# Third layer's edge stage: where VectorE reads an item's tile number, and which join releases the buffer of item records

## The chip, the cores and the metric

The kernel runs on one core of one Trainium2 chip. The metric is the device time of one execution in microseconds. A core has five engines that run side by side and synchronise by semaphores: TensorE (PE in the profile), VectorE (DVE), ScalarE (ACT), GpSimd (POOL) and SyncE (SP). In the stage of this case SP and POOL are used for starting transfers: SP starts plain ones, POOL the indirect ones (gathers), whose row addresses come from an index column in SBUF.

## The reference

The model is a graph network of four layers over 6250 nodes and 100000 edges, 128 features to a node. Each layer's output is added to its input and normalised. The case touches the third layer, of which only the edge part matters here:

```
row, col = edge_index
h = concatenate([x[row], edge_attr], axis=1)      # per edge: 128 + 128 features
h = relu(h @ w1a + b1a)                           # 256
h = relu(h @ w1b + b1b)                           # 256
h = h @ w1c + b1c
summed = segment_sum(h, col, num_segments=n)      # per node
```

The last product is linear, so the kernel sums the second hidden layer over the edges of a node first and multiplies by `w1c` in a later stage. The first product is split too: the part of `x` stands ready in one table (`table_layer2`, 256 values to a node), the part of `edge_attr` in another (`hidden_edge_parts`), and an edge only adds two rows.

## The kernel before

The edges are sorted by target node and laid out in *items*. An item holds up to four edges (S = 4) for each of 128 partitions, and a partition stands for one node of a tile of 128 nodes; all 128 nodes belong to tile number `j`, which the item's record carries in column `R_J`. The record (20 integers to a partition) also holds the indices of the item's gathers. The running sums of all 50 tiles lie in SBUF (`total`), and an item adds into the part of its tile. The stage goes through the items in a loop; a turn has U = 8 items, and the trip count is read at run time.

An item passes through five steps. In the text, "item g" counts from zero over all turns.

- **Fetch** (SP, L1992). The records of four items (called a *half-turn* below: a turn has two, `q` = 0 and 1) come in one transfer of 40 KB into `rec[q]`. There are two such buffers. The fetch for a buffer waits until the buffer is released.
- **Gather** (POOL, L2009 and L2014). One indirect DMA brings the edge parts of the item (`gh`, a ring of NH = 4 buffers), four more bring the node parts (`gx`, a ring of 8). Before the five, POOL waits for the record's fetch, for `turned` (the transposes of item g-8) and for `joined` (the join of item g-4).
- **Join** (DVE, L2081, helper `join`). Four additions of 128x256: `gx` += `gh`. It waits for the item's five gathers, and then increments `joined`.
- **Transposes, relu, layer 2** (PE L2035 in `turn_over`, ACT L2064 in `relu1`, PE L2045 in `layer2`). PE's order is the transposes of item g+1, then the four products of item g. PSUM has two buffers for each of the two steps, and so has `h1`.
- **Sum** (DVE, L2101). Eight `scalar_tensor_tensor` of 128x128 (max with minus the bias, then add to the running sum of tile `j`). DVE's order in the loop is: join of item g+2, read of item g's tile number into a register (`value_load`, L2096), wait for item g's products (`lin2`), sum of item g, and after the fourth item of a half-turn the release `rec_free[q]`.

The order on each queue is written out by hand; no planner is involved. The counters start above zero (`joined` by U, `turned` by U, `summed` and `act1` by 2) so that first uses of a ring pass.

Of the kernel before, what the change touches and what calls it, by code (L numbers as in the profile page):

```python
# [16 lines left out]
NT = -(-N // P)  # L17
# [7 lines left out]
U = 2 * B  # L25
# [28 lines left out]
R_POS, R_J, R_LIFT, R_SUM, FW = 0, 1, 2, 3, 4  # L54
# [12 lines left out]
def gnn(nc, xT, src, dst, windows, edges, W0, W0T, attI, attJ, probs, importance, bias0,  # L67
        Ws, WsT, Wd, WdT, attS, attD, bias1, bias1cols, w1a, b1a, w1b, b1b, w1cT, b1c, w2a, b2a, w2b, b2b,
        w3T, out):
    fp32, bf16, i32, u32, u16 = (mybir.dt.float32, mybir.dt.bfloat16, mybir.dt.int32, mybir.dt.uint32,  # L70
                                     mybir.dt.uint16)
    ALU, ACT, AX = mybir.AluOpType, mybir.ActivationFunctionType, mybir.AxisListType
    ds = bass.ds
    V, A, PE, G = nc.vector, nc.scalar, nc.tensor, nc.gpsimd
# [18 lines left out]
    with top:  # L93
        def sb(name, shape, dt=fp32, ctx=top):
            return ctx.enter_context(nc.sbuf_tensor(name, shape, dt))
# [6 lines left out]
        def sem(name):  # L102
            live.append(nc.alloc_semaphore(name=name))
            return live[-1]
# [18 lines left out]
        def flat(ap):  # L123
            return ap.rearrange("p a c -> p (a c)")
# [27 lines left out]
        with ExitStack() as ph:  # L152
            def carve(of, at, shape, dt=fp32):
                size = 1
                for k in shape:
                    size *= k
                words = size if dt in (fp32, i32, u32) else -(-size // 2)
                v = of[:, at:at + words]
                if dt is not fp32:
                    v = v.bitcast(dt)  # L160
                names = "abcd"[:len(shape)]
                v = v[:, 0:size].rearrange(f"p ({' '.join(names)}) -> p {' '.join(names)}", **dict(zip(names, shape)))
                return v, at + words
# [15 lines left out]
            for v in range(2):  # L179
                cbuf.append([])  # L180
                for half in range(2):
                    c, at = carve(pool1, at, [CB, REC], i32)
                    cbuf[v].append(c)
            fbuf = []
            for v in range(2):
                fbuf.append([])
                for half in range(2):
                    c, at = carve(pool1, at, [CB + IPC, REC], i32)
                    fbuf[v].append(c)
            we = []  # L190
            for v in range(2):
                c, at = carve(pool1, at, [QG, 2 * WIN], i32)
# [4 lines left out]
            for q in range(2):  # L197
                c, at = carve(pool2, at, [EC], i32)
# [65 lines left out]
            for v in range(STG):  # L264
                c, at = carve(flat(xr[:, :, :]), at, [T4, A0P])
                stage.append(c)
                c, at = carve(flat(xr[:, :, :]), at, [OWN])
# [576 lines left out]
        def turns(eng):  # L844

            return eng.value_load(trips[0:1, 0:1], min_val=1, max_val=GMAX // U - 7)
# [368 lines left out]
        with ExitStack() as att:  # L1215
# [10 lines left out]
            def room(at, *shape):  # L1226

                size = 1
                for k in shape:
                    size *= k  # L1230
                names = "abcd"[:len(shape)]
                v = big[:, at:at + size].rearrange(f"p ({' '.join(names)}) -> p {' '.join(names)}",
                                                   **dict(zip(names, shape)))
                return v, at + size
# [224 lines left out]
            for v in range(2):  # L1459
                c, at = room(at, H * (C + 1), SLOTS + 1)  # L1460
# [32 lines left out]
            for v in range(2):  # L1493
                c, at = room(at, CHUNKS[0], HID)
# [460 lines left out]
            with ExitStack() as ph:  # L1955
                NH, NQ = 4, 2
                Q = U // NQ
                rec = [sb(f"rec_m{q}", [P, Q, REC], i32, ph) for q in range(NQ)]
                gx, gh, h1, at = [], [], [], 0
                for u in range(U):  # L1960
                    v, at = room(at, S, HID)
# [4 lines left out]
                for v in range(2):  # L1966
                    c, at = room(at, 2 * S * P)
# [2 lines left out]
                psX = [pb(f"psX{v}", [P, 2 * 512], fp32, ph) for v in range(2)]  # L1970
                ps2 = [pb(f"ps2_{v}", [P, 2 * 512], fp32, ph) for v in range(2)]
                rec_in = [sem(f"rec_in_m{q}") for q in range(NQ)]
                rec_free = [sem(f"rec_free_m{q}") for q in range(NQ)]
                gathered = [sem(f"gathered_m{u}") for u in range(U)]
                gate, gate_v = sem("gate_m"), sem("gate_mv")
                joined = sem("edge_parts_added_m")
# [7 lines left out]
                def following(i, u):  # L1984

                    return (i, u + 1) if u < U - 1 else (i + 1, 0)

                @block.sync
                def _(sp):
                    def fetch(i, q):  # L1990
                        sp.wait_ge(rec_free[q], i + 1)
                        sp.dma_start(rec[q][:, :, :], rec_d[:, ds(i * U + q * Q, Q), :]).then_inc(rec_in[q], 16)  # L1992

                    n = turns(sp)
                    with sp.Fori(0, n) as i:
                        for q in range(NQ):
                            fetch(i, q)
                    fetch(n, 0)
# [74 lines left out]
                @block.vector  # L2073
                def _(dve):
                    def join(i, u):

                        dve.wait_ge(gathered[u], (i + 1) * 16 * (S + 1))
                        x_, e_ = flat(gx[u][:, :, :]), flat(gh[u % NH][:, :, :])
                        for s in range(S):
                            at = slice(s * HID, (s + 1) * HID)  # L2080
                            last = V.tensor_tensor(x_[:, at], x_[:, at], e_[:, at], ALU.add)  # L2081
                        last.then_inc(joined, 1)

                    for c in rec_free:
                        dve.sem_inc(c, 1)
                    dve.sem_inc(summed, 2)
                    dve.sem_inc(joined, U)
                    n = turns(dve)
                    join(0, 0)
                    join(0, 1)  # L2090
                    with dve.Fori(0, n) as i:
                        for u in range(U):
                            g, q = i * U + u, u // Q
                            join(*following(*following(i, u)))
                            dve.sem_inc(gate_v, 1)
                            j = dve.value_load(rec[q][0:1, u % Q, R_J:R_J + 1], min_val=0, max_val=NT)  # L2096
                            dve.wait_ge(lin2, g + 3)
                            for s in range(S):
                                for f in range(2):
                                    t = total[:, ds(j, 1), f, :].rearrange("p a n -> p (a n)")  # L2100
                                    V.scalar_tensor_tensor(t, ps2[u % 2][:, (f * S + s) * P:(f * S + s + 1) * P], nbb[:, f:f + 1], t,  # L2101
                                                           ALU.max, ALU.add)
                                last = V.drain()
                            last.then_inc(summed, 1)
                            if u % Q == Q - 1:
                                dve.sem_inc(rec_free[q], 1)

            fresh_semaphores()
            added = [sem(f"added_{s}") for s in range(S)]
# [1 line left out]
            with ExitStack() as ph:  # L2111
# [3 lines left out]
                for v in range(2):  # L2115
                    c, at = room(at, TB, P)
                    xd.append(c)
                    c, at = room(at, TB * P)
                    xdT.append(c)
                    c, at = room(at, 2, TB * P)  # L2120
# [174 lines left out]
        with ExitStack() as ph:  # L2295
            w3 = sb("w3T_", [P, D], fp32, ph)
            rec = [sb(f"rec_s{u}", [P, S, FW], i32, ph) for u in range(U)]
# [118 lines left out]
            with ExitStack() as fi:  # L2416
                FT = 7
                GF = groups(NT, FT)
                q = [[sb(f"q{v}{s}", [P, FT, D], fp32, fi) for s in range(S)] for v in range(2)]
# [226 lines left out]
```

## Time and profile before

| quantity | value |
|---|---|
| median of 3 runs | 8602.15 us (8601.02 to 8606.16) |
| span of the profiled execution | 9989.8 us |
| time of the profiled execution itself | not given beside the span |
| the stage of this case in the profile | 6224 to about 8160 us of the span |
| mean granted TensorE clock, whole span | 0.653 |
| busy in the span | PE 47%, DVE 51%, ACT 15%, POOL 58% |

The profiled execution is 1388 us longer than the median run, so a microsecond of the profile isn't a microsecond of the metric. The stage has 57 fetches, which makes 28 turns, 56 half-turns and 224 items. Slices 25 to 32 of the page's forty hold the stage. A granted clock of 1.0 is 2.4 GHz on TensorE, 0.5 is 1.2 GHz. "Idle before <-releaser" in a row is the time in which an engine did nothing before the instruction, and the program's name for what ended it; it is inferred from semaphore events, and "remote" or a transfer that ended long ago stands where no fitting event was found.

### The profile page before, as it was taken

The page shows a single profiled execution, that of the slowest core. Times are in us where ns is not written, and L with a number is a line of the kernel's source. Part 1 is how long each engine was busy: PE and PEld are TensorE (multiplying, and loading weights), DVE is VectorE, ACT ScalarE, POOL GpSimd, SP SyncE. Part 2 cuts the span into 40 slices and gives each one's busy share as a digit, 9 for nine tenths or more (in the row PEclk, how much of TensorE's full clock was granted, in tenths as well). Part 3 has the DMA queues.
Part 4 walks back from the last instruction along what each step waited for, and adds up shares of the span by engine and source line. Part 5 has one row for each costly group of instructions (what it writes and reads, how often), then busy time and mean ns, then how long its engine had stood idle before and what let it go on. Part 6 is the DMA issues. An engine that isn't in the chain of part 4 may idle for free. (4 is left out here: it accounts for less than half of the span.)

```text
span 9989.8 us, 82305 instructions
## 1 busy us (share of the span) xinstructions
PE 4658.3 (47%) x14536; PEld 2840.5 (28%) x14536; DVE 5136.0 (51%) x11795; ACT 1546.3 (15%) x3063; POOL 5819.3 (58%) x5427
## 2 busy tenths in 40 slices
PE   6287777733233322222322225566666566444443
PEld 5133333222222212221222122333333333333332
DVE  6387787755555444544454454444444433333333
ACT  1211111121111211111211112111111112000002
POOL 2466666536666466656466562555555534888885
PEclk8688888855555655555555555778778786555555
DMA  2432323443333233333333332444444441444445
GB/s 68 126 61 55 56 57 56 50 112 85 83 82 86 71 84 83 93 86 83 77 89 87 86 89 62 123 123 127 125 122 128 123 80 24 36 36 36 36 36 100
DMA packets 658400, 804.99 MB, mean 81 GB/s; under 512 B 289379, under 2 KB 496662, under 8 KB 657175
## 3 DMA queue, kind: packets, MB, share of 16 engines
q0 software_dynamic: 317424, 531.92, 26.9%
q1 hardware_dynamic: 340902, 272.29, 9.0%
q8 instruction: 22, 0.36, 0.0%
q14 instruction: 52, 0.42, 0.0%
HBM read 575.15 MB, written 228.61 MB: 80 GB/s over the span
## 5 line engine op out<-in xcount | busy, mean ns | idle before, releaser
L1767 POOL DMA_INDIRECT big<-table_layer,slot_records_L x2400 | 2325.7, 969 | 1615.9 <-DMA slot_records_L<-slot_records 861.3
L1786 PE MATMUL own_ps_L<-of_tile_L,big 50*128 50x16 f32 x1224 | 284.0, 370 | 2804.4 <-DVE fade_L L1871 2522.3
L2408 POOL DMA_INDIRECT sums_by_source<-msg,to x800 | 1252.4, 1565 | 260.7 <-issue 189.4
L981 POOL DMA_INDIRECT big<-table_layer,idx_L x912 | 951.1, 1043 | 619.5 <-issue 285.8
L2045 PE MATMUL ps<-big,w 128*128 128x512 f32 x1792 | 957.9, 685 | 341.6 <-ACT big L2064 208.4
L1786 PEld LDWEIGHTS own_ps_L<-of_tile_L,big 50*128 50x128 f32 x1224 | 272.0, 324 | 2879.5 <-issue 2865.1
L2014 POOL DMA_INDIRECT big<-table_layer,rec_m x904 | 877.5, 971 | 275.4 <-issue 272.0
L2101 DVE SCALAR_TENSOR_TENSOR big<-ps,nbb,big 128x128 f32 x1792 | 545.8, 346 | 914.0 <-remote 658.9
L1057 PE MATMUL sums_L<-h,ident 128*128 128x512 f32 x1344 | 716.4, 683 | 188.9 <-DVE h L1137 166.6
L1893 DVE TENSOR_TENSOR_SCAN big<-h,products_L 128x1122 f32<-128x1122 f32 x300 | 747.6, 2492 | 24.6
L2350 PE MATMUL psM<-h,same 128*128 x1600 | 413.8, 440 | 643.2 <-issue 640.1
L1778 PE MATMUL psH_L<-w,h 128*128 128x256 f32 x1584 | 671.8, 607 | 25.4 <-DMA h<-in_edges 25.4
L1844 DVE TENSOR_SCALAR of_tile_L<-slot_records_L,place 50x16 f32<-50x16 int32 x153 | 35.2, 230 | 1218.2 <-DMA slot_records_L<-slot_records 1128.6
L2009 POOL DMA_INDIRECT big<-hidden_edge_parts,rec_m x226 | 216.0, 956 | 688.0 <-DMA rec_m<-item_records 230.6
L1884 DVE TENSOR_TENSOR products_L<-products_L,big 128x512 f32<-128x512 f32 x600 | 613.5, 1067 | 0.0
L2045 PEld LDWEIGHTS ps<-big,w 128*128 128x128 f32 x1792 | 381.5, 225 | 766.9 <-issue 652.1
L2350 PEld LDWEIGHTS psM<-h,same 128*128 128x128 f32 x1600 | 355.9, 327 | 711.3 <-issue 711.3
L1778 PEld LDWEIGHTS psH_L<-w,h 128*128 128x128 f32 x1584 | 488.8, 319 | 138.0 <-issue 25.6
L2064 ACT ACTIVATE big<-psX 128x1024 f32<-128x1024 f32 x225 | 228.5, 1024 | 1704.5 <-DMA b<-in_b2b 1073.1
L1826 ACT ACTIVATE big<-psH_L 128x1536 f32<-128x1536 f32 (+1 forms) x144 | 193.7, 1345 | 1811.7 <-DMA h<-in_edges 860.0
L1057 PEld LDWEIGHTS sums_L<-h,ident 128*128 128x128 f32 x1344 | 289.5, 221 | 622.6 <-issue 606.3
L2035 PE MATMUL psX<-ident,big 128*128 128x128 f32 x1800 | 283.4, 308 | 391.9 <-DVE big L2081 303.4
(440 smaller groups left out, 7501.0 us busy)
## 6 DMA issues: line engine op xcount, KB each, us to landing
hidden_edge_parts<-big SPq DMA_DIRECT2D x72, 768.0 KB
hidden_edge_parts<-big SPq DMA_DIRECT2D x72, 640.0 KB
big<-table_layer,slot_records_L POOLq DMA_INDIRECT x2400
h<-in_edges SPq DMA_DIRECT2D x75, 384.0 KB
h<-in_edges SPq DMA_DIRECT2D x72, 320.0 KB
table_layer<-xr SPq DMA_DIRECT2D x49, 298.0 KB
big<-table_layer,idx_L POOLq DMA_INDIRECT x912
big<-table_layer,rec_m POOLq DMA_INDIRECT x904
```

The costliest lines, as they stand in the source:

```text
L981: G.indirect_dma_start(out=g[b][:, u, s, :], out_offset=None, in_=table, in_offset=bass.IndirectOffsetOnAxis(ap=at, axis=0)).then_inc(gath ...
L1057: PE.matmul(sums[b][u][:, 0:T * D], ident[:, :], prod[PROD[u]][:, s, :], start=(s == 0), stop=False, skip_group_check=True)
L1767: G.indirect_dma_start(out=ring[b][:, s, :], out_offset=None, in_=tab1_d[l], in_offset=bass.IndirectOffsetOnAxis(ap=fl[q][:, at + s, R_POS ...
L1778: last = PE.matmul(psH[:, c * HID:(c + 1) * HID], eT[b % 2][:, c * P:(c + 1) * P], w1[:, 1, :], start=True, stop=True)
L1786: last = PE.matmul(own_ps[:, c * SLOTS:(c + 1) * SLOTS], own1T[:, c * P:(c + 1) * P], of_tile[b % 2][:, :], start=True, stop=True)
L1884: last = V.tensor_tensor(p4[:, c, 0:C, 1:SLOTS + 1], bc(wt[:, hd, :], 1, C), ring[b][:, :, hd * C:(hd + 1) * C].rearrange("p s c -> p c s" ...
L1893: V.tensor_tensor_scan(flat(tot[b % 2][:, rows, :]), flat(shrink[:, rows, :]), flat(prod[:, :, :]), 0.0, ALU.mult, ALU.add)
L2014: G.indirect_dma_start(out=gx[u][:, s, :], out_offset=None, in_=tab2_d, in_offset=bass.IndirectOffsetOnAxis(ap=rec[q][:, a, s * FW + R_POS ...
L2045: last = PE.matmul(ps2[u % 2][:, f * S * P:(f + 1) * S * P], w2[:, k, f * P:(f + 1) * P], h1[u % 2][:, k * S * P:(k + 1) * S * P], start=( ...
L2101: V.scalar_tensor_tensor(t, ps2[u % 2][:, (f * S + s) * P:(f * S + s + 1) * P], nbb[:, f:f + 1], t, ALU.max, ALU.add)
L2350: last = PE.matmul(psM[v][:, s * P:(s + 1) * P], same[v][:, s, :], flat(h[:, ds(js[s], 1), :]), start=True, stop=True)
L2408: G.indirect_dma_start(out=sum_d[s], out_offset=bass.IndirectOffsetOnAxis(ap=to[u][:, s:s + 1], axis=0), in_=msg[u][:, s, :], in_offset=No ...
```

## The change

Each join copies the item's tile number out of the record into a small tile of its own (`tile`, one row of 8 integers), and the `value_load` before the sum reads that copy. The record is thereby no longer read after the join. The two `rec_free` semaphores go away. SP's fetch for buffer `q` of turn `i` now waits on `joined` for the fourth join of the items that used the buffer before. (`joined` starts at 8, so the count `i*U + q*Q + Q` is that of the join of item `(i-1)*8 + q*4 + 3`.) One drain of DVE stands between the first two joins and the loop.

```diff
                 rec = [sb(f"rec_m{q}", [P, Q, REC], i32, ph) for q in range(NQ)]
+                tile = sb("tile_m", [1, U], i32, ph)
...
-                rec_free = [sem(f"rec_free_m{q}") for q in range(NQ)]
...
                     def fetch(i, q):
-                        sp.wait_ge(rec_free[q], i + 1)
+                        sp.wait_ge(joined, i * U + q * Q + Q)
                         sp.dma_start(rec[q][:, :, :], rec_d[:, ds(i * U + q * Q, Q), :]).then_inc(rec_in[q], 16)
...
                         x_, e_ = flat(gx[u][:, :, :]), flat(gh[u % NH][:, :, :])
+                        V.tensor_copy(tile[:, u:u + 1], rec[u // Q][0:1, u % Q, R_J:R_J + 1])
                         for s in range(S):
...
-                    for c in rec_free:
-                        dve.sem_inc(c, 1)
                     dve.sem_inc(summed, 2)
                     dve.sem_inc(joined, U)
                     n = turns(dve)
                     join(0, 0)
                     join(0, 1)
+                    dve.drain()
                     with dve.Fori(0, n) as i:
                         for u in range(U):
-                            g, q = i * U + u, u // Q
+                            g = i * U + u
                             join(*following(*following(i, u)))
                             dve.sem_inc(gate_v, 1)
-                            j = dve.value_load(rec[q][0:1, u % Q, R_J:R_J + 1], min_val=0, max_val=NT)
+                            j = dve.value_load(tile[:, u:u + 1], min_val=0, max_val=NT)
...
                             last.then_inc(summed, 1)
-                            if u % Q == Q - 1:
-                                dve.sem_inc(rec_free[q], 1)
```

## Rows read from the trace of the kernel before

**Rows 1.** Windows view of the stage: its length, then busy time and count by engine.

```profile
core 0: us, PE busy (x) PEld busy (x) DVE busy (x) ACT busy (x) POOL busy (x), PEclk, DMA share, GB/s
6224.00:8170.00 1946.00, 1209.55 (x3614) 610.97 (x3614) 871.19 (x2704) 230.49 (x229) 1095.93 (x1135) 0.79 0.45 123
```

**Rows 2.** Waits of POOL in the stage: total us, times, longest us.

```profile
POOL big L2014 <- issue: 272.0, 893, 0.3
POOL big L2009 <- DMA rec_m<-item_records: 230.6, 25, 11.6
POOL big L2009 <- DVE big L2081: 211.0, 25, 9.1
POOL big L2009 <- PE psX L2035: 58.9, 5, 22.0
```

**Rows 3.** Groups of instructions by line in the stage (busy us, mean ns | idle before).

```profile
L2014 POOL DMA_INDIRECT big<-table_layer,rec_m x904 | 877.5, 971 | 275.4 <-issue 272.0 <-PE psX L2035 2.4 <-DVE big L2081 0.9
L2101 DVE SCALAR_TENSOR_TENSOR big<-ps,nbb,big 128x128 f32 x1792 | 545.8, 346 | 914.0 <-remote 658.9 <-PE ps L2045 166.2 <-issue 39.1
L2009 POOL DMA_INDIRECT big<-hidden_edge_parts,rec_m x226 | 216.0, 956 | 688.0 <-DMA rec_m<-item_records 230.6 <-DVE big L2081 211.0 <-issue 187.5
```

**Rows 4.** Timeline of one half-turn: start us, duration us, engine, line, operation [idle before].

```profile
6904.96 34.60 SPq L1992 DMA_DIRECT2D rec_m<-item_records  x2
6907.81 0.95 POOL L2009 DMA_INDIRECT big<-hidden_edge_parts,rec_m  x1 [9.06 <-DMA rec_m<-item_records]
6908.12 5.62 PE L2045 MATMUL ps<-big,w 128*128 128x512 f32 x8
6909.00 1.43 DVE L2081 TENSOR_TENSOR big<-big 128x256 f32<-128x256 f32 x4
6909.07 1.18 POOL L2014 DMA_INDIRECT big<-table_layer,rec_m  x1 [0.31 <-issue]
...
6913.91 2.66 DVE L2101 SCALAR_TENSOR_TENSOR big<-ps,nbb,big 128x128 f32 x8 [3.48 <-PE ps L2045]
...
6918.35 1.09 PE L2035 MATMUL psX<-ident,big 128*128 128x128 f32 x8 [0.29 <-DVE big L2081]
6919.27 3.60 PE L2045 MATMUL ps<-big,w 128*128 128x512 f32 x8
6919.30 2.66 DVE L2101 SCALAR_TENSOR_TENSOR big<-ps,nbb,big 128x128 f32 x8 [1.09 <-issue]
6919.60 0.95 POOL L2014 DMA_INDIRECT big<-table_layer,rec_m  x1 [0.30 <-issue]
...
6922.33 1.43 DVE L2081 TENSOR_TENSOR big<-big 128x256 f32<-128x256 f32 x4 [0.37 <-DMA big<-table_layer,rec_m]
...
6930.49 1.02 ACT L2064 ACTIVATE big<-psX 128x1024 f32<-128x1024 f32 x1 [14.81 <-DMA b<-in_b2b]
...
6932.46 0.96 POOL L2014 DMA_INDIRECT big<-table_layer,rec_m  x1 [0.31 <-issue]
6936.23 1.03 ACT L2064 ACTIVATE big<-psX 128x1024 f32<-128x1024 f32 x1 [4.72 <-DMA b<-in_b2b]
6936.27 2.66 DVE L2101 SCALAR_TENSOR_TENSOR big<-ps,nbb,big 128x128 f32 x8 [12.51 <-remote]
...
6941.78 0.95 POOL L2009 DMA_INDIRECT big<-hidden_edge_parts,rec_m  x1 [8.36 <-DVE big L2081]
```

**Rows 5.** Waits over the whole span, those on TensorE's results without a fitting releaser.

```profile
ACT big L2064 <- DMA b<-in_b2b: 1073.1, 87, 29.8
ACT big L1826 <- DMA h<-in_edges: 860.0, 48, 19.8
ACT big L1826 <- remote: 636.9, 39, 19.4
```

**Rows 6.** Instructions by line: the read of the tile number, and a DVE operation on one column.

```profile
L2096 DVEq TENSOR_LOAD <-rec_m x224: 298/302/318, 6247.7 to 8154.7; - x112
L2168 DVE TENSOR_SCALAR spare<-place x1: 140/140/140, 8160.4 to 8160.4; 128x1 f32<-128x1 f32 x1
```

## The prediction

> **What bounds the kernel now.** I looked at the windows first, to see the stage by itself: about 1940 us of the profiled span, with PE busy 1210, DVE 871 and POOL 1096 [rows 1]. No engine is full, so the next view is the waits of the engine that feeds the others. POOL starts 1130 gathers at 0.97 us each, with 0.305 us of issue between two (272.0 over 893) [rows 2, 3]. That is 1130 x 1.273 = 1438 us of work that can't be overlapped. The rest of the stage is POOL idle ahead of an item's first gather: 230.6 + 211.0 + 58.9 = 500 us [rows 2]; 1438 + 500 is the stage. There are 55 places between two half-turns, so some 9 us of pause stand in each.
>
> The timeline shows what a pause is [rows 4]. POOL starts the gathers of a half-turn at 6907.81 and ends the twentieth at 6933.42 (25.6 us). The next one starts at 6941.78, after 8.36 us. The two fetches in the view start 34.60 us apart, at 6904.96 and about 6939.2. Each is released by the sum of the fourth item of an earlier half-turn; here that sum starts at 6936.27, so it is the late part. It had waited 12.51 us. Its join was over at 6923.76, and the products that it needs (6919.27, 3.60 us) are drawn as ended at 6922.87. So the row says that DVE waited 12.5 us for something drawn as done. ACT does the same: transposes drawn as ended at 6919.44 release it at 6930.49. In total 658.9 us of DVE's waits at the sum are of this kind, 83 of them [rows 3].
>
> In the profile, then, the loop is: late products, fourth sum, fetch, pause of POOL. The question on which the prediction turns is whether the lateness exists in a plain run. The profiled span is 9989.8 us, and a plain run takes 8602.15: 1388 us are the profile's own, and they must lie somewhere. Late completions of TensorE are the best candidate, for two reasons. The same odd waits stand in another stage that has TensorE beside transfers (860.0 and 636.9 us at L1826) and in this one (1073.1 at L2064) [rows 5]. And TensorE has by far the most instructions here, 3614 loads and 3614 products beside 2704 on DVE and 1135 on POOL [rows 1], so whatever recording costs hits it first. The Trainium skill (Perfetto Trace Analysis, Per-instruction lifecycle) says that a TensorE row's end is estimated and not observed. By that the products may really have ended at 6936, which speaks for the second rival below; it doesn't tell whether a plain run has them so late.
>
> **The stage in a plain run, if the lateness is the profile's.** From the start of a half-turn's gathers (6907.81 = 0) by the rows [rows 4]: the join of its second item ends at 23.76 - 7.81 = 15.95. The fourth sum of the half-turn before may follow at once and takes 2.7: 18.7. The fetch that it releases brings POOL back to work after 6941.78 - (6936.27 + 2.66) = 2.85: 21.5. POOL itself is busy to 25.6 + 0.3 = 25.9. So the fetch is hidden with 4.4 us to spare, and the stage is POOL's 1438 us with or without the change. But TensorE counts: at the low clock transposes and products of an item take longer (5.62 beside 3.60 for the eight rows). Transposes at 10.5, then 2.0 and 6.8 (twice 1.09 and 3.60, less what overlaps), end the products at 19.3, the sum at 22.0 and the restart at 24.9: 1.0 us to spare, and none if TensorE comes into the half-turn with work left over. Also the fetch of the rows runs with no gather on the way, which wouldn't hold in a plain run.
>
> **The change part by part.**
> - *Release at the fourth join.* That join has ended at 6909.00 + 1.43 = 6910.43, 2.6 us after the start, where the fourth sum in the profile is done at 6938.9. With 2.85 us to the restart the record is there at 5.5, against 25.9 when POOL wants it: 20 us of cover, and no state of TensorE's clock can use it up. What is late next for POOL is the join of item g-4 (ended at 6918.21, so 10.4 against 25.9) and the transposes of item g-8. The join stands in DVE's queue behind the sum of item g-7, so TensorE's lateness still reaches POOL, though with three items of slack in place of one or two. Gain in a plain run: the low clock was granted in 2 x (1 - 0.79) = 0.42 of the stage [rows 1]; in these half-turns, 0.42 x 56 = 24, I take a remaining pause of 1 us, from 1.0 to spare less leftovers and the fetch's slower way: 24 us less 2 for what stays, 22. Bounds: 0 (always hidden), and the whole 500 less the first 22.0, about 480.
> - *The copy in the join.* 224 + 2 copies of one integer. The nearest row is 0.14 us [rows 6]: 32 us of DVE, which is idle for over 900 us of the stage [rows 3]. The copy comes before the additions, so it delays the join by up to 0.14, which eats into covers of 15 and 20 us. Nothing on POOL's path; if the cover is gone, 32 us. I take 0, since there is no gain to be had from it, and no wait is added.
> - *Reads from the copy.* The same load, 0.30 us in DVE's queue [rows 6], under the join's 1.43: 0.
> - *`rec_free` out, drain in.* Two increments a turn less (0.02 us class of instruction, not on a path), one drain in all: 0 within 1 us.
> - *SP.* The fetch's instruction moves forward and nothing is queued behind it but the next fetch. Its 40 KB come among gathers now, which take 0.45 of the transfer engines' time [rows 1]: a slower transfer, under 20 us of cover.
>
> There is one thing on the copy which a page has otherwise. In the rows a gather that meets a join takes 1.18 us rather than 0.95 [rows 4], so the two engines do get in each other's way. The Trainium skill (SBUF — State Buffer, SBUF: two separate sides) says that a DVE copy within SBUF can hold the ports that GpSimd needs to write descriptors, for its whole duration. As a mechanism here: each copy would hold POOL for its 0.14 us, 226 x 0.14 = 32 us, and POOL is the bound.
>
> Sum: 0.42 x 56 x 1 - 2 = 22 us less, all of it a plain run's time. 8602 - 22 = 8580.
>
> **The rivals.**
> 1. *All hidden already.* POOL never waits for a record in a plain run. For it: 4.4 us to spare at the high clock. Against: little to spare at the low one. Time 8602.
> 2. *TensorE is late in plain runs too, and by the transfers.* In the rows the last products are seen 3 us after POOL's last gather, so perhaps they come through only when the gathers have ended. Then unbroken gathers make TensorE the bound. From 6907.81 to 6936.27 three items got through, 9.5 us each, where the loop now needs 34.6 / 4 = 8.65. With no pause all 224 run at 9.5: 0.85 x 224 = 190 us slower, 8790. It decides if an item's products take over 8.65 us while gathers run. This is the slower side.
> 3. *The pauses are real, and lateness has nothing to do with the gathers.* Then the early fetch takes out a good part of 500 us. If everything, 8602 - 480 = 8122; if TensorE takes up most of it (busy 1210 plus a late 10 us each half-turn), some 2 to 4 us a pause go, 110 to 220 us: 8440.
> 4. *The copy is paid by POOL.* 32 us more on top of either of the first two: 8612 or 8634.
>
> **How the numbers follow.** Forecast (a remainder of pause goes, 8557 to 8592): 0.40. Rival 1: 0.32. Rival 3 in part: 0.10; whole: 0.06. Rival 4: 0.08. Rival 2: 0.04. A measurement of this kernel tells about 0.2%, 17 us, from no change. Faster: 0.32 of the forecast's 0.40 (a gain over 17), and rival 3: 0.48. Same: 0.08, rival 1, and half of rival 4: 0.44. Slower: the rest, 0.08. The range 8470 to 8625 holds the forecast, rival 1, most of rival 4 and the lower part of rival 3, some 0.8. The likeliest case's own range is 8557 to 8592.
>
> **What would show it.** In the profile after, SP's fetch follows the fourth join, some 28 us before POOL needs the record, and the wait `DMA rec_m` of 230.6 us is gone. If late completions are the profile's, the profiled stage needn't get shorter in proportion: POOL's idle time will be moved to waits for a join or for the transposes, and DVE's `remote` waits stay. A profiled stage near 1450 us with POOL gapless and a plain time near 8122 would show rival 3; gathers unbroken, POOL waiting on joins, and a plain time above 8625 rival 2. Gathers longer than 0.97 us in the mean by 0.03 or more would show rival 4. The forecast is wrong if the plain time moves by more than 45 us either way.

## The result, and the profile after

The kernel after takes 8671.6 us in the median (four runs, 8669.5 to 8675.1), the kernel before 8604.2 (8601.0 to 8616.3). The ratio is 1.0075 with a 95% interval of 1.0063 to 1.0086: slower by 0.75%, 67 us between the medians. The forecast was 8580, and the time lies outside the range of 8470 to 8625.

The profile of after has a span of 8673.4 us, which is its plain time. So a profile lengthens the run little or not at all (in the sets below the profiled run lies 0.2% from the median at most), and the profile of before with its 9989.8 us was no inflated picture of an 8602 us run; it was a picture of another one. The experiments showed what it most likely was: on one chip the kernel before takes 10106 us in the median of 17 runs, on two others 8598 to 8602. The times on record are of the second kind; the profile that the prediction read looks like the first, with the same waits. Its "late products" are real there and absent here. The rows of before that the rows of after should be held against are therefore those of a later profile of the unchanged kernel (e13), with a span of 8615.3 us.

First the windows view of the stage, kernel before and kernel after, on the kind of chip that counts. The columns are as in [rows 1].

```profile
5312.00:6800.00 1488.00, 1114.45 (x3632) 569.00 (x3632) 860.46 (x2704) 234.15 (x232) 1100.12 (x1135) 0.92 0.59 161
```

```profile
5309.00:6850.00 1541.00, 1125.16 (x3604) 571.07 (x3604) 866.69 (x2930) 231.87 (x228) 1172.05 (x1135) 0.91 0.57 156
```

Against [rows 1] the granted clock is 0.92 and not 0.79, and the stretch that holds the stage is 458 us shorter. Between the two fences one number moves with the time: POOL's busy time, 1100 to 1172 us for the same 1135 instructions. PE and DVE move by 11 and 6 us.

POOL's waits, before (first fence) and after (second), answer to [rows 2]:

```profile
POOL big L2014 <- issue: 269.3, 884, 0.3
POOL big L2009 <- issue: 204.8, 224, 136.7
POOL big L2009 <- DMA rec_m<-item_records: 14.3, 1, 14.3
```

```profile
POOL big L2014 <- issue: 273.3, 897, 0.3
POOL big L2009 <- issue: 204.3, 226, 135.8
```

Here the 500 us of [rows 2] have shrunk to one pause of 14.3 us (the 136 of L2009 is the wait ahead of the stage). That one is gone after: the early release does what it says. Now the groups by line, before and after, for [rows 3]:

```profile
L2014 POOL DMA_INDIRECT big<-table_layer,rec_m x904 | 882.1, 976 | 275.4 <-issue 269.3 <-DVE big L2081 2.7 <-PE psX L2035 2.1
L2101 DVE SCALAR_TENSOR_TENSOR big<-ps,nbb,big 128x128 f32 x1792 | 544.6, 345 | 123.2 <-PE ps L2045 68.7 <-issue 5.1
L2081 DVE TENSOR_TENSOR big<-big 128x256 f32<-128x256 f32 x904 | 326.0, 423 | 491.3 <-DMA big<-table_layer,rec_m 487.1 <-issue 2.2
```

```profile
L2014 POOL DMA_INDIRECT big<-table_layer,rec_m x904 | 954.1, 1055 | 275.5 <-issue 273.3 <-DVE big L2082 1.2 <-PE psX L2035 0.9
L2101 DVE SCALAR_TENSOR_TENSOR big<-ps,nbb,big 128x128 f32 x1792 | 542.4, 343 | 95.3 <-PE ps L2045 44.9
L2082 DVE TENSOR_TENSOR big<-big 128x256 f32<-128x256 f32 x904 | 318.3, 405 | 0.0
L2079 DVE COPY tile_m<-rec_m 1x1 int32<-1x1 int32 x226 | 32.0, 142 | 576.7 <-DMA big<-table_layer,rec_m 574.0 <-issue 0.8
```

The 904 gathers of node parts cost 72 us more: 976 to 1055 ns. The additions of the joins became *shorter*, 423 to 405 ns, though they still start 0.335 us apart. Something has changed in the join itself, and it was worth looking at single gathers. The account of the stage: from the first to the last of these gathers it takes 1453.6 us before (5317.3 to 6770.9) and 1511.4 after (5313.6 to 6825.0), 57.8 more, which is 72.0 of longer gathers less 14.3 of the pause. The two spans differ by 58.1 us, so the rest of the kernel plays no part.

The timeline shows how one gather gets long. In both kernels a join starts just ahead of a gather; before first, then after (columns as in [rows 4]).

```profile
5491.36 1.43 DVE L2081 TENSOR_TENSOR big<-big 128x256 f32<-128x256 f32 x4 [4.71 <-DMA big<-table_layer,rec_m]
5491.52 1.10 POOL L2014 DMA_INDIRECT big<-table_layer,rec_m  x1 [0.30 <-issue]
```

```profile
6017.67 0.14 DVE L2079 COPY tile_m<-rec_m 1x1 int32<-1x1 int32 x1 [4.72 <-DMA big<-table_layer,rec_m]
6017.74 1.41 DVE L2082 TENSOR_TENSOR big<-big 128x256 f32<-128x256 f32 x4
6017.82 2.17 POOL L2014 DMA_INDIRECT big<-table_layer,rec_m  x1 [0.30 <-issue]
```

Undisturbed, a gather takes 0.95 us. Before, this one loses 0.15 us. Its additions start at 0.00, 0.34, 0.68 and 1.01 of the join, the gather at 0.16; it gets on at the start of the second. After, it loses 1.22 us: from 6017.82 to about 6019.1, when the sum behind the fourth addition starts (6019.08). Both fit one picture: something early in a gather (an estimate from starts and losses: 0.04 us after its start) has to wait while DVE runs a join; with nothing ahead of the additions it gets in at the next start of one, 0 to 0.3 us later, and with the copy directly ahead it gets in only when all four are over.

That holds for most gathers and not for all. After, 198 of the 226 joins meet a gather that starts ahead of the fourth addition. In 175 of them the gather is held until all four are over, in 22 it gets in at an earlier start, and in one it loses nothing. One of the 22:

```profile
5426.75 0.14 DVE L2079 COPY tile_m<-rec_m 1x1 int32<-1x1 int32 x1 [0.21 <-DMA big<-table_layer,rec_m]
5426.82 1.41 DVE L2082 TENSOR_TENSOR big<-big 128x256 f32<-128x256 f32 x4
5427.66 1.06 POOL L2014 DMA_INDIRECT big<-table_layer,rec_m  x1 [0.30 <-issue]
```

This gather starts 0.84 us into the additions and loses 0.11 us, so it got in at the fourth. The difference seems to be VectorE's idle time ahead of the copy: 0.12 to 0.21 us in 21 of the 22, and 0.3 us or more in all 175. The traces of e5, e6 and e15 have the same split (after a short idle time 49 early and 5 held, after a longer one 1 early and 525 held). No run was made to test it, and it isn't a rule for every instruction: with the maximum of e8, 17 of 18 gathers were held after a short idle time too.

Gathers above 1.0 us number 101 of 1130 before and 221 after. In after, 156 of them lose 0.25 to 0.45 us, because 131 of the 226 joins start 0.2 to 0.3 us into a gather, so that the next one starts late in the join. A join is mostly woken by the landing of a gather (201 joins of before waited for one), which would explain why the phase repeats.

### The profile page after: what moved, and what is told of

It is laid out like the page before. It is cut to its first block and busy times, and to the rows that moved or that the text cites. A ratio compares the mean times of both kernels' runs of the same rounds, so it can differ in the third digit from the quotient of the medians.

```text
span 8673.4 us, 82502 instructions
## 1 busy us (share of the span) xinstructions
PE 4544.4 (52%) x14536; PEld 2796.5 (32%) x14536; DVE 5139.1 (59%) x12021; ACT 1537.5 (18%) x3063; POOL 5909.7 (68%) x5427
## 5 line engine op out<-in xcount | busy, mean ns | idle before, releaser
L981 POOL DMA_INDIRECT big<-table_layer,idx_L x912 | 975.4, 1070 | 405.3 <-issue 293.2
L2014 POOL DMA_INDIRECT big<-table_layer,rec_m x904 | 954.1, 1055 | 275.5 <-issue 273.3
L2045 PE MATMUL ps<-big,w 128*128 128x512 f32 x1792 | 890.9, 644 | 0.0
L2045 PEld LDWEIGHTS ps<-big,w 128*128 128x128 f32 x1792 | 359.0, 211 | 374.8 <-issue 374.8
L1856 DVE TENSOR_TENSOR z_L<-own_ps_L,big 128x64 f32<-128x64 f32 x150 | 39.2, 261 | 679.0 <-DMA big<-table_layer,slot_records_L 679.0
L2390 DVE TENSOR_TENSOR to<-away,rec_s 128x4 uint32<-128x4 f32 x200 | 33.1, 165 | 670.9 <-POOLq L2405 668.3
L1137 DVE TENSOR_TENSOR h<-sc_L,big 128x512 f32<-128x512 f32 x672 | 422.5, 689 | 0.0
```

Source lines behind the costliest of these rows:

```text
L981: G.indirect_dma_start(out=g[b][:, u, s, :], out_offset=None, in_=table, in_offset=bass.IndirectOffsetOnAxis(ap=at, axis=0)).then_inc(gath ...
L2014: G.indirect_dma_start(out=gx[u][:, s, :], out_offset=None, in_=tab2_d, in_offset=bass.IndirectOffsetOnAxis(ap=rec[q][:, a, s * FW + R_POS ...
L2045: last = PE.matmul(ps2[u % 2][:, f * S * P:(f + 1) * S * P], w2[:, k, f * P:(f + 1) * P], h1[u % 2][:, k * S * P:(k + 1) * S * P], start=( ...
```

## The experiments

| run | what it is | this, us | before beside it, us | ratio (95%) |
|---|---|---|---|---|
| e1 | before | 10110 (one) | 10106 | |
| e2 | copy, late release | 10112 | 10106 | 1.0005 (0.9987 to 1.0024) |
| e3 | early release, copy on ScalarE | 10030 | 10106 | 0.9907 (0.9882 to 0.9933) |
| e4 | after, second copy | 9950 | 10106 | 0.983 (0.980 to 0.986) |
| e5 | after | 8655.7 | 8601.8 | 1.0058 (1.0041 to 1.0074) |
| e6 | as e2 | 8663.7 | 8601.8 | 1.0067 (1.0050 to 1.0083) |
| e7 | as e3 | 8593.1 | 8601.8 | 0.9992 (0.9982 to 1.0001) |
| e8 | maximum in place of the copy | 8668.6 | 8601.8 | 1.0073 (1.0056 to 1.0090) |
| e9 | copy, drain, additions | 8606.2 | 8597.8 | 1.0012 (1.0003 to 1.0022) |
| e10 | additions, then copy | 8588.5 | 8597.8 | 0.9990 (0.9980 to 1.0000) |
| e11 | copy ahead of the wait | 8587.0 | 8597.8 | 0.9991 (0.9981 to 1.0000) |
| e12 | one copy per half-turn | 8609.0 | 8597.8 | 1.0014 (1.0005 to 1.0024) |
| e13 | before | 8617 (one) | 8599.1 | |
| e14 | before, memset written ahead of the additions | 8598.9 | 8599.1 | 1.000 (0.999 to 1.001) |
| e15 | after | 8660.9 | 8599.1 | 1.0072 (1.0055 to 1.0089) |
| e16 | as e11 | 8592.8 | 8599.1 | 0.9990 (0.9980 to 0.9999) |

Runs e1 to e4 were made on the chip where before takes 10106 us, the other twelve on two chips where it takes 8600 (e5 to e12 on one, e13 to e16 on the other).

**Taking the change apart.** Copy without release (e2, e6; the drain ahead of the loop is in them too, and left out in e3 and e7):

```diff
                         x_, e_ = flat(gx[u][:, :, :]), flat(gh[u % NH][:, :, :])
+                        V.tensor_copy(tile[:, u:u + 1], rec[u // Q][0:1, u % Q, R_J:R_J + 1])
...
-                            j = dve.value_load(rec[q][0:1, u % Q, R_J:R_J + 1], min_val=0, max_val=NT)
+                            j = dve.value_load(tile[:, u:u + 1], min_val=0, max_val=NT)
```

Release without a copy on VectorE (e3, e7), against the kernel after:

```diff
-                        V.tensor_copy(tile[:, u:u + 1], rec[u // Q][0:1, u % Q, R_J:R_J + 1])
...
+                        if u % Q == 0:                        # in relu1, ScalarE
+                            act.wait_ge(rec_in[q], (i + 1) * 16)
+                            A.activation(tile[:, q * Q:(q + 1) * Q], rec[q][0:1, :, R_J], ACT.Copy).then_inc(tiled, 1)
...
+                            if u % Q == 0:
+                                dve.wait_ge(tiled, i * NQ + u // Q + 1)
```

and a second copy into an unread tile (e4). On the first chip:

> The kernel before, unchanged, for a profile whose own time agrees with the plain time. Theory A (the copy keeps POOL from writing descriptors): the stage takes about 1470 us, POOL has no pause between half-turns, and its gathers take 0.96 to 0.97 us in the mean, so that all of them together are some 70 us shorter than in the kernel after (1.055 us for those of the node parts). Theory B (gathers are longer because nothing interrupts them, or because the fetch goes out among them; the copy is innocent): the gathers are short here only where POOL pauses, so pauses of one or more us stand between half-turns.

> The copy and the read from it as in the kernel after, but the buffer of records is released by the fourth sum, as before. Theory A: all of the loss is here, 8672 us (+0.8%), with gathers as long as after. Theory B: 8604 us, as before.

> The early release as in the kernel after, but the tile numbers are copied by ScalarE, one instruction of four numbers to a half-turn; VectorE does no copy. Theory A: the loss is gone, 8595 to 8606 us, gathers 0.97 us in the mean. Theory B: 8672 us as after, since the release is early here too.

> The kernel after with a second copy of the same number into a tile that nobody reads, behind the first. Theory A: POOL is held longer, by at least 0.14 us an item where a gather is under way: 8695 to 8740 us. Theory B: 8672 us, as after.

None of the times of theory A or B came out, since they were worked out for 8604 us and the kernel before takes 10106 here. But this chip is the one whose kind the first profile showed, so its rows can be held against [rows 2]. POOL's waits of the kernel before (e1), then of e3, then of e4:

```profile
POOL big L2009 <- DVE big L2081: 245.1, 27, 9.4
POOL big L2009 <- DMA rec_m<-item_records: 240.9, 26, 10.9
```

```profile
POOL big L2010 <- DVE big L2086: 400.4, 69, 10.6
```

```profile
POOL big L2010 <- DVE big L2084: 220.8, 30, 10.3
```

The pauses are there in e1, 486 us of these two waits. In e3 the wait for the record is gone, but the wait for a join has grown from 245 to 400 us, and the kernel is 76 us faster. The join stands behind a sum in VectorE's queue, and the sum waits for TensorE, so this is where the lateness would come back; it was argued from the code and not tested. With release and two copies (e4) the kernel is 156 us faster than before, although its gathers of node parts take 967.3 us against 881.6 in e1. The copy alone (e2) costs nothing that shows. POOL has slack here, and the copy also does less: the gathers are only 15 us longer than in e1 (896.5 us), as in 160 of e2's 226 joins the copy follows a sum within 0.25 us, the case in which few gathers are held. Why TensorE's results come late on this chip, and why e4 gains more than e3, I can't say; nothing was run for it, and the kernel after itself was not run on such a chip.

On the second chip:

> The kernel after, unchanged. The first four runs showed the kernel before at 10106 us on their chip, where the times on record are 8604 (before) and 8672 (after). Theory A with a second part (on a chip where TensorE's results come late, POOL pauses, and the early release helps; on one where they don't, POOL never pauses and only the copy's cost is left): where the kernel before takes 8604, this takes 8672; where it takes 10106, this takes 30 to 150 us less than before. Theory B: 0.8% slower on either.

> The copy and the read from it, with the release by the fourth sum as before. Theory A: where the kernel before takes 8604, this takes 8665 to 8680, with POOL's gathers 75 us longer in all; where before takes 10106, the same as before. Theory B: as before on either.

> The early release, with the tile numbers copied by ScalarE. Theory A: where the kernel before takes 8604, this takes 8590 to 8606 and its gathers 0.96 to 0.97 us in the mean; where before takes 10106, 10030 as it did. Theory B: 8672 on the first kind of chip.

On this chip the loss goes with the copy, as theory A has it, and B falls: the copy alone carries the whole loss (+62 us, e6, with 958.3 us for the 904 gathers), the early release alone gives 9 us (e7), with an interval that touches no change. In e7 nothing interrupts the gathers either, and the 904 take 883.4 us, so theory B's reason for longer ones is out. Of the times, e5 came out 16 us below what theory A gave and e6 1 us below its range. What A says of the kernel after on the slower chip stays untested.

**What kind of instruction.** e8 puts a maximum of the number with itself in the copy's place; e14 puts a memset there, in the kernel before.

```diff
-                        V.tensor_copy(tile[:, u:u + 1], rec[u // Q][0:1, u % Q, R_J:R_J + 1])
+                        r = rec[u // Q][0:1, u % Q, R_J:R_J + 1]
+                        V.tensor_tensor(tile[:, u:u + 1], r, r, ALU.max)
```

```diff
+                        V.memset(tile[:, u:u + 1], 0)
                         for s in range(S):
```

> The kernel after with a two-input maximum of the number with itself in place of the copy: same size, same place, another kind of instruction. Theory A in its narrow form (only a copy takes the second pair of ports that GpSimd writes its descriptors through): where before takes 8604, this takes 8600 to 8615. Theory A in its wide form (any instruction ahead of the additions lengthens what VectorE runs without a break, and gathers wait for its end): 8660 to 8680.

> The kernel before with one thing more: a memset of one integer of a tile that nobody reads, directly ahead of the four additions; release and read of the tile number are untouched. Theory C: it is enough that a short instruction runs straight into the additions, whatever it reads: 8655 to 8680 us where before takes 8600. Rival E: the instruction has to read SBUF (the copy and the maximum do): 8600 to 8612. Where before takes 10100, no difference that the intervals can tell.

The maximum costs what the copy costs (+67 us, gathers 961.2 us in all), so it isn't a matter of copies. The memset costs nothing, and the additions and the gathers keep their old length:

```profile
L2015 POOL DMA_INDIRECT big<-table_layer,rec_m x904 | 879.6, 973 | 275.5 <-issue 267.9 <-DMA rec_m<-item_records 3.7 <-DVE big L2083 3.0
L2083 DVE TENSOR_TENSOR big<-big 128x256 f32<-128x256 f32 x904 | 324.4, 421 | 482.2 <-issue 482.2
```

So theory C, by which any short instruction there is enough, was too wide. But e14 isn't as clean a test of rival E as it was meant to be. The profile doesn't draw the memset ahead of the additions:

```profile
5475.48 0.42 DVE L2083 TENSOR_TENSOR big<-big 128x256 f32<-128x256 f32 x1 [4.45 <-issue]
5475.49 0.06 DVE L2080 MEMSET tile_m<- 1x1 int32 x1
5475.53 1.19 POOL L2015 DMA_INDIRECT big<-table_layer,rec_m  x1 [0.30 <-issue]
```

In 189 of the 226 joins the memset starts 0.01 us behind the first addition, in the other 37 0.01 us ahead of it. The copy and the maximum start 0.07 us or more ahead of it in every join. So either the instruction has to read SBUF (rival E), or it only has to hold the additions back by its 0.07 us; these runs don't tell the two apart.

**Where it stands.** e9 puts `dve.drain()` between copy and additions, e10 moves the copy behind the additions (it then increments `joined`), e11 and e16 move it ahead of the wait for the gathers, e12 copies four numbers at once in the first join of a half-turn.

```diff
+                        dve.wait_ge(rec_in[u // Q], (i + 1) * 16)
+                        V.tensor_copy(tile[:, u:u + 1], rec[u // Q][0:1, u % Q, R_J:R_J + 1])
                         dve.wait_ge(gathered[u], (i + 1) * 16 * (S + 1))
                         x_, e_ = flat(gx[u][:, :, :]), flat(gh[u % NH][:, :, :])
-                        V.tensor_copy(tile[:, u:u + 1], rec[u // Q][0:1, u % Q, R_J:R_J + 1])
```

> The kernel after with a drain between the copy and the four additions. The traces so far (before at 8602 on that chip) show a gather that starts during a join waiting for the next start of an addition where nothing stands ahead of them, and for the end of all four where a copy or a maximum stands directly ahead. Theory C (what counts is that the small instruction runs straight into the additions, which then give no opening to POOL): with the drain between them the gathers go back to 0.97 us in the mean; 8590 to 8615 us where before takes 8602. Theory D (the small instruction costs POOL by itself, or its presence in the join does): 8655 to 8680, as after.

> The kernel after with the copy behind the four additions instead of ahead of them (it carries the increment of joined). Theory C: nothing stands ahead of the additions, so 8590 to 8620 us where before takes 8602, unless the sum that may follow straight after the copy takes its place. Theory D: 8655 to 8680.

> The kernel after with the copy ahead of the wait for the gathers, so that VectorE's idle time (208 of 226 joins in the kernel after have one, 2.8 us in the mean) lies between copy and additions. Theory C: 8590 to 8612 us where before takes 8602. Theory D: 8655 to 8680.

> The kernel after with one copy of four numbers in a half-turn's first join, none in the other three. Both theories: a quarter of the loss, on top of what the early release gives (8593 with the copy on ScalarE): 8593 + 65 / 4 = 8609, 8603 to 8620 us where before takes 8602. If the price went by something else than the number of joins that have a copy, it would stay near 8660.

All four speak for theory C and against D; e9 and e12 lie in C's ranges, e10 and e11 1.5 and 3 us below them. The same copy of the same number costs 65 us directly ahead of the additions and nothing elsewhere (e10, e11). With one drain it costs 8 us against before, 18 against the 8588 of the early release without a price, and the gathers don't go all the way back to 0.97 us (0.99 for those of the node parts). In one join of four it costs 11 and 21 us, some more than the quarter of 65 that was expected. The gathers account for both: 895.2 us in e9 and 898.5 in e12, against 878.9 in e11. Rows of e9, then of e16:

```profile
6001.58 0.14 DVE L2079 COPY tile_m<-rec_m 1x1 int32<-1x1 int32 x1 [2.20 <-DMA big<-table_layer,rec_m]
6001.79 1.43 DVE L2083 TENSOR_TENSOR big<-big 128x256 f32<-128x256 f32 x4
6002.63 1.09 POOL L2014 DMA_INDIRECT big<-table_layer,rec_m  x1 [0.30 <-issue]
```

```profile
L2014 POOL DMA_INDIRECT big<-table_layer,rec_m x904 | 879.2, 973 | 275.6 <-issue 267.7 <-DVE big L2083 6.7 <-PE psX L2035 1.2
L2083 DVE TENSOR_TENSOR big<-big 128x256 f32<-128x256 f32 x904 | 325.1, 421 | 404.9 <-DMA big<-table_layer,rec_m 404.4
```

In e9 the additions start 0.21 us after the copy rather than 0.07, take 1.43 us again and not 1.41, and the gather that meets them loses 0.14 us. The join has moved against the gathers by that delay, so more of them (191 above 1.0 us, against 105 in e11) meet an addition and lose such a small amount.

The traces of e11 also say something on the exception above. In 24 of its joins VectorE was so late that the copy ran straight into the additions after all. The additions are short there, but VectorE had hardly been idle ahead of the copy, and not one gather was held to the end.

**Repeats.**

> The kernel before, unchanged, once more for a profile. Where it takes 8600: no pause of POOL but one or two at the start (in the kernel with the copy alone, which has the same release, they add up to 13 us), gathers of 0.97 us in the mean, the stage's first to last gather in 1445 to 1460 us. If pauses stand between the half-turns all along, the early release should have given more than the 9 us that it gave with the copy on ScalarE, and theory C lacks a part. Where it takes 10100: as in the first profile.

> The kernel after, unchanged. Where before takes 8600: 8655 to 8675 as on record. Where before takes 10100 (TensorE's results late, POOL pausing at each half-turn): 9950 to 10080, faster than before, since the early release with the copy on ScalarE gave 75 us there and the release with two copies 156.

> The version that came out best: early release, copy ahead of the wait for the gathers. Where before takes 8600: 8580 to 8600, and faster than the kernel after by 60 to 85 us. Where before takes 10100: 10000 to 10060, like the copy on ScalarE.

e13 gave the rows of before shown above: one pause of 14.3 us and none at the half-turns. e15 confirms the loss (1.0072), e16 the best version: the early release with the copy ahead of the wait takes 0.1% less than before in two sets of runs (intervals 0.9981 to 1.0000 and 0.9980 to 0.9999, so at the edge of no difference), and 68 us less than after. It is the change as it was meant, without its price.

## Why the prediction was wrong

- **"Nothing on POOL's path; if the cover is gone, 32 us. I take 0"** is the step that failed. The prediction put the copy's cost on VectorE, where idle time hides it, and its upper bound at 226 x 0.14 = 32 us. It measured 62 us (e6 against before), with 76 us of longer gathers (958.3 us against 882.1). The bound was worked out from the copy's own length, while what POOL waits for is the copy and the four additions behind it, 1.48 us as drawn, from wherever in them the gather starts. Rival 4 had the right engine and the right sign of evidence (gathers longer by 0.03 us or more: 0.079) but half the price, and got 0.08.
- The prediction saw a gather of 1.18 us that met a join [rows 4] and took it as proof of a small toll. It should have asked what decides how long the toll is. The Trainium skill (SBUF — State Buffer, SBUF: two separate sides) says that the port pair which DVE and GpSimd share is locked for a full instruction, and that a DVE instruction with two SBUF inputs takes part in it against a GpSimd instruction that reads SBUF. By that rule the toll ends with the addition under way, and the rows of before agree (0 to 0.3 us). With the copy ahead it lasted over four additions, up to 1.3 us, which the rule doesn't have; there the measurement decides.
- **The early release: 22 us forecast, 9 measured** (e7, interval -1 to 16). The term "1 us of pause in 24 half-turns" was mis-sized; it came from a TensorE at the low clock in 0.42 of the stage. On the chips that count the granted clock of the stage is 0.92, and there was no pause at any half-turn; what was won is the one pause of 14.3 us while the pipeline fills, which the prediction didn't name.
- **"1388 us are the profile's own"** was wrong: a profile costs 0.2% at most here (8673.4 beside 8671.6). The inference drawn from it, that a plain run has no late products and that POOL bounds the stage at 1438 us, came out all the same (1453.6 us from first to last gather, no `remote` wait left on DVE). That was luck: it holds because the times came from another chip than the profile, and on the chip of the first profile it would have failed. The gap between the profile's span and the median could have said that the two were of different chips, or of a chip in different conditions; it was read as a cost of recording, which nothing in the profile spoke for.
- Rivals: 1 (all hidden) describes the release nearly as well as the forecast. 2 didn't occur. 3 is the world of the other chip, and even there only 76 of 486 us came, as the wait for the join grew. Above the measured time lay only rival 2 with its 8790, by another mechanism; with the copy on POOL's path the prediction went no higher than 8634.
- Right: the copy's own 0.14 us (0.142), the read from the copy and SP's earlier fetch among gathers at no cost that shows (e7 and e11 have both and are no slower than before), POOL as the bound.

## What to carry to other kernels

Where POOL bounds a stage by starting gathers, an instruction on VectorE isn't free because VectorE is idle: look at what the gather that meets it waits for, and price it by the whole run of instructions from there on. A short VectorE instruction like this copy belongs ahead of a wait or behind the long ones, not directly ahead of them. And when a profile's span differs by 16% from the times beside it, treat its pauses as those of another machine until a profile with a matching span has been seen.

## What the runs showed of the hardware that was not expected

- With a copy or a maximum of one element directly ahead of four 128x256 additions, an addition takes 405 ns in the mean rather than 421 to 423, and a gather that starts under them is mostly held until the last is over (175 of 198 joins in after; up to 2.24 us for one that takes 0.95). With nothing, a drain or idle time ahead of the additions, or with a memset written there, it gets in at the start of the next addition. The shorter mean shows that the small instruction runs straight into the additions; it doesn't show by itself that a gather was held, as the 22 exceptions of after have short additions too.
- One chip runs the same kernel at 10106 us and two others at 8600, each steadily. On the slower one TensorE's results reach the other engines long after the drawn end: in the half-turn of [rows 4] the sum starts 13.4 us after it, and 2.9 us after POOL's last gather has ended. On the faster ones no such wait is left. What differs between the chips wasn't found.
